# The expert loop of a fused convolution-attention and mixture-of-experts kernel: the small product that moves the second expert's doubled rows, issued in front of the late piece instead of behind it

## The reference

```
x = x + xattn(layernorm(x), k, bias, ctx, ctx, 8)      # long convolution over 512 positions, by head
x = x + moe(layernorm(x))

def moe(x):                                            # T = 512-wide rows
    scores = softmax(xf @ gate_w.T)                    # 64 experts
    topk_w, topk_idx = top_k(scores, 6)
    # each expert gets up to CAP = 128 of the tokens that chose it (gx), in order
    g, u = split(gx @ gate_up_proj)                    # 512 -> 2 * 192
    eo = (silu(g) * u) @ down_proj * buf_w             # 192 -> 512
    routed = zeros.at[buf_tok].add(eo)                 # rows added at their token
    shared = silu(xf @ sg.T) * (xf @ su.T) @ sd.T      # on all tokens, 384 wide
    return routed + shared
```

## Time and profile before

| | |
|---|---|
| time, median of 3 runs | 1144.73 us (1144.46 to 1146.67) |
| the profiled execution, its own time | 1139.92 us |
| its span in the trace | 1137.9 us |
| TensorE products, busy | 1070.9 us, 94% |
| TensorE weight loads, busy | 840.7 us, 74% |
| VectorE, busy | 825.4 us, 73% |
| GpSimd, busy | 744.1 us, 65% |
| ScalarE, busy | 527.3 us, 46% |
| the two products of `c_move` (line 699) | 64 instructions, 390 ns each in the median |
| the late pieces (lines 626 and 640) | 240 and 90 instructions |

### The profile page before, as it was taken

How to read it: one execution, slowest core, us unless ns; L and a number is a source line. 1 busy time by engine, 2 the same in 40 slices (tenths; PEclk the granted TensorE clock), 3 DMA queues, 4 the chain that set the end, 5 groups by cost and what they waited for, 6 DMA issues and landing times.

```text
span 1137.9 us, 17561 instructions
## 1 busy us (share of the span) xinstructions
PE 1070.9 (94%) x5077; PEld 840.7 (74%) x5077; DVE 825.4 (73%) x1414; ACT 527.3 (46%) x951; POOL 744.1 (65%) x436
## 2 busy tenths in 40 slices
PE   3999999999999999999889999999999999999790
PEld 2777777777777778778789998777777776777460
DVE  3799999999999999999589983465555565555360
ACT  4565556556655655564314222444444444444240
POOL 6999999999999999998012333344345435443432
PEclk9999999999999999999999999999999999999895
DMA  6365644554555445552585556899999999999874
GB/s 195 111 175 161 170 129 138 159 164 133 139 161 160 136 140 161 154 147 79 160 238 136 135 140 170 249 291 294 269 301 290 296 281 267 295 276 278 216 177 60
DMA packets 91134, 217.08 MB, mean 191 GB/s; under 512 B 11240, under 2 KB 15656, under 8 KB 90961
## 3 DMA queue, kind: packets, MB, share of 16 engines
q1 hardware_dynamic: 74544, 177.75, 52.7%
q0 software_dynamic: 16544, 38.78, 16.3%
HBM read 164.82 MB, written 52.18 MB: 191 GB/s over the span
## 4 chain that ended last, share of the span: by engine, by line
PE 72%; DMA 15%; issue 4%; POOL 2%; ACT 1%; DVE 1%; POOLq 0%; DVEq 0%; ACTq 0%
PE Y L460 11%; PE Y L462 11%; PE Y L461 11%; PE Y L547 8%; PE Y L667 7%; PE Y L464 5%; DMA out_dram<-pT,idx_i 4%; DMA out_dram<-o,idx_i 4%; DMA out_dram<-w,idx_i 4%; PE DX L483 2%; PE DX L565 2%; PE Y L626 2%; PE OT L565 2%; PE DX L690 2%; PE TA L477 1%
## 5 line engine op out<-in xcount | busy, mean ns | idle before, releaser
L1032 POOL TENSOR_TENSOR ring<-vT,pT 128x1024 f32<-128x1024 f32 x128 | 249.9, 1963 | 11.1 <-ACT vT L783 10.9
L460 PE MATMUL Y<-split,toep 128*128 128x512 f32 x576 | 237.8, 413 | 10.2 <-POOL split L1040 10.2
L1040 POOL TENSOR_TENSOR split<-ring,split 128x1024 fp32r<-128x1024 f32 x96 | 231.7, 2413 | 0.0
L462 PE MATMUL Y<-split,toep 128*128 128x512 f32 x576 | 226.9, 394 | 0.0
L461 PE MATMUL Y<-split,toep 128*128 128x512 f32 x576 | 225.7, 392 | 0.0
L667 PE MATMUL Y<-ring,xT 128*128 128x384 f32 x512 | 190.8, 496 | 0.0
L1207 DVE TENSOR_TENSOR z<-Y,cT 128x1024 f32<-128x1024 f32 x128 | 156.9, 1226 | 26.9 <-PE Y L464 26.1
L1213 DVE TENSOR_REDUCE o<-z 128x128 f32<-128x1152 f32 x128 | 172.2, 1345 | 1.2
L460 PEld LDWEIGHTS Y<-split,toep 128*128 128x128 f32 x576 | 108.8, 189 | 30.6 <-issue 7.9
L789 ACT ACTIVATE split<-ring 128x1024 fp32r<-128x1024 f32 x96 | 100.8, 1050 | 58.8 <-POOL ring L1032 58.8
L462 PEld LDWEIGHTS Y<-split,toep 128*128 128x128 f32 x576 | 108.5, 188 | 24.3
(11 more groups left out here) (163 smaller groups left out, 1878.3 us busy)
## 6 DMA issues: line engine op xcount, KB each, us to landing
ring<-_L_ffn_gate_up_proj_dram SPq DMA_DIRECT2D x64, 768.0 KB
ring<-in_L_ffn_down_proj_dram SPq DMA_DIRECT2D x64, 384.0 KB
gr<-filters SPq DMA_DIRECT2D x32, 512.0 KB, 4.1
stage<-in_x_dram SPq DMA_DIRECT2D x32, 256.0 KB, 5.6
pT<-in_turned_dram SPq DMA_DIRECT2D x32, 256.0 KB, 4.3
cT<-in_turned_dram SPq DMA_DIRECT2D x32, 256.0 KB, 4.2
xr<-in_x_dram SPq DMA_DIRECT2D x32, 256.0 KB, 3.8
xn_rows<-xn SPq DMA_DIRECT2D x32, 256.0 KB, 2.9
```

Of the source, the lines that this page charges most:

```text
L460: pe.matmul(y, high, kv[:, s, 0, a, n], start=(a == 0), stop=False)
L462: last = pe.matmul(y, low, kv[:, s, 0, a, n], start=False, stop=(a == c))
L1032: pool.tensor_tensor(to.rearrange("p (b j i) -> p b j i", i=NH, j=NH), a, d, ALU.mult).then_inc(kvp_ready, 1)
L1040: pool.tensor_tensor(kv[:, s, 1, c, :], kvp[c], kv[:, s, 0, c, :].bitcast(F32), ALU.subtract).then_inc(kv_ready, 1)
```

## The change

In TensorE's `c_iteration`, the call of `c_move` is taken from behind the late piece to in front of it. Nothing else is changed: same instructions, same waits, same buffers, on all engines.

```diff
@@ -711,14 +711,14 @@
                 if e:
                     c_turn_hid(e - 1)
                 c_up(e, 1)
+                if e % 2 and e > 1:
+                    c_move(e // 2 - 1)
                 if part == "gate":
                     late_half(t, 0)
                 if part == "up":
                     late_half(t, 1)
                 if part == "out":
                     late_out(t)
-                if e % 2 and e > 1:
-                    c_move(e // 2 - 1)
                 if e:
                     c_out(e - 1)
                 if turns(e):
```

## The result

Twelve runs of the changed kernel have a median of 1142.27 us (1139.02 to 1146.83), twelve of the kernel before 1142.05 us (1135.85 to 1151.77). The means, 1142.4 and 1142.1 us, are no further apart than the medians, so these runs by themselves show no difference. The comparison of the runs gives a ratio of 1.0059, with a 95% interval of 1.0036 to 1.0083: slower by 0.6%. The ratios compare fast runs only, and a run more than 1.5% above the fastest of its kernel doesn't count as one, so in the second series the 10 longest of the 35 runs of the kernel before are left out and none of the changed one's; over all its runs the medians give 1.0047 and the means 1.0057.

The account below looks back on a forecast made before the run. TensorE's pace, held at times by the add chain, bounds stage C; 21.0 us of waits less 11.0 of gather waits moves TensorE's end 10.0, the last add 3.8; with the chain's 0 to 7.3, +4 us: 1148.7, range 1143.5 to 1153.0.

Parts of the forecast that it names:

- What bounds the kernel: Stage C: TensorE sets the pace, the scatter-add chain holds it at times and ends last.
- The wait: TensorE's move waits for VectorE's low part of the second expert's result: 0.78 us in 27 iterations, 21.0 us.
- The second way of counting: Wait on TensorE from pair periods, 10.71 less 10.08 us: 0.63 us each, 17.0 in all, the low end.
- The rule of the Trainium skill on weight loads pulled ahead of products: TensorE could pull a load ahead of each of 27 waits; the row was against it, so nothing was subtracted.
- The 11.0 us of gather waits go: TensorE's waits for gathered tokens, 9.6 and 1.4 us, vanish because slower TensorE no longer catches up with the add chain.
- +10.0: TensorE's end in stage C moves later by 21.0 - 11.0 = 10.0 us.
- +3.8: By TensorE's path, the last pair's first add goes out at 1127.0 against 1123.18, 3.8 us later.
- The path by the add chain: Scatter-adds from pair 23 on: last pair's first add 0 to 7.3 us late, middle near TensorE's path.
- The sum on the median: The 4 us taken for the profiled execution was put on the median of runs too, giving 1148.7 us.
- rival (2): TensorE's slack hides all waits, result within 0.2%: 0.63 us a wait, end -0.2 us, 1144.5; chance 0.23.
- (1): The add chain ends last, with the 29.07 us and three full pairs: +7.3 us, 1152; chance 0.23.
- (3): Faster: slower TensorE absorbs the add chain's lateness and thinner traffic shortens the chain, 1143.7 or 1141.5 us; chance 0.09.
- (4): The 27 short waits make TensorE's clock fall to 1.2 GHz at times: +10 us or more, 1155; chance 0.03.

Follow-up runs that it names:

- second series: The unedited changed kernel timed again beside the kernel before: 1142.18 against 1136.84 us, ratio 1.0093 (1.0065 to 1.0121).
- profile pair: One profiled execution of each kernel: the changed one took 1139.02 us, 0.9 us less than the one of before.
- second profile of the changed kernel: A further profiled execution of the unedited changed kernel, from its repeat timing: 1147.78 us.
- second half alone: Against the kernel before, the move stands in front of the piece only in iterations 29 to 55 (14 of 27): 1134.81 us, ratio 0.9968.
- first series: The first timing, twelve runs of each kernel: changed 1142.27 us, before 1142.05 us, ratio 1.0059 (1.0036 to 1.0083).
- old order with (3, 6): Kernel before, third group of shared tiles not added in the loop, four tiles added at the end: 1135.79 us, ratio 0.9963.

## Why the prediction was right, and where it was off

- **What bounds the kernel.** Right. TensorE's pace with holds by the add chain is what the runs show: without the adds of nine shared tiles the kernel takes 1122 us, 12.7 less than with them, and its trace has no wait for gathers.
- **The wait, 0.78 us in 27 iterations, 21.0 us.** The mechanism was right in each of the 27, the size a quarter too large: 0.62 and 16.8 us, 0.60 and 16.3 where nothing else holds TensorE. The mis-sized term is the one read from weight loads' starts, without the 0.16 that the work behind gives back. The second way of counting, 0.63 from the period of pairs, stood in the text as the low end and was close. The lesson is to price a wait by the period of the whole loop where both kinds of iteration are in the trace, not by one gap.
- **The rule of the Trainium skill on weight loads pulled ahead of products** ("TensorE: Matmul & The Clock Gate", "Step-by-step: what each phase is for"). The traces after agree with what was taken from the row: the waiting move's loads start at 925.00, 0.12 us behind the low part's end at 924.88. They aren't pulled ahead of the wait.
- **The 11.0 us of gather waits go.** Right in the profile pair; in the second profile of the changed kernel one of 1.9 us is left. TensorE's last move went from 1114.07 to 1119.58, +5.5 where I had +10.0. The smaller wait accounts for 4.2 of the difference. Two more errors nearly cancel: by the distances of its moves the kernel before had lost 12.4 us, not 11.0, and the loop began 1.3 us later in the changed one. The last pair's first add went from 1123.18 to 1122.60, -0.6 where I had +3.8.
- **The path by the add chain.** The term "if the shared tiles' adds behind it take what they took (29.07)" was mis-sized: they took 22.3 us, 7 less, where I had allowed for 6% less. Pair 23's add was at 1032.55 and not 1034.8. These 7 us go far to explain why the chain was not late at the end of that profile. In the second profile it was, by 8.9 us.
- **The sum on the median.** That +4 came near is partly luck. The profiled pair, for which the sum was made, came out at -0.9 us, as rival (2) had it with its 0.63 a wait (TensorE's end +6.0, the end -0.2). The median of the second series came out at +5.3. The step between the two, "I put the same 4 us on it", has no reason in the trace, and no run shows it: how far an execution's waits for the chain hide the change varies from run to run. An error in the wait and one in this step had opposite signs.
- **Rivals.** (1), the chain late by 7 us at the end, didn't come in the first profile (1.1 us) and came in the second (8.9 us), the run of 1147.78 us. (2), all hidden, holds for the profile pair and for the second half alone, and by the medians for the first series, not for the second. (3) was refuted: the fastest run of the changed kernel, 1138.32, is above 61 of the 105 runs of before. (4): the granted clock stayed at 1.00 in the windows from 731 to 1107.

## What to carry to other kernels

A wait that is set in front of covering work costs its length in every round when the path to it starts at the waiting engine itself. If another chain holds that engine now and then, the cost is hidden in part: take the other chain away in an experiment, and the whole price appears (17.3 us here, against 5). Where runs spread by 2%, one profile isn't the mean: two profiles of the same changed kernel have the last adds 1.1 and 8.9 us late. And where they spread unequally, look at what a ratio of selected runs left out.

## What was not expected of the hardware

- Most of the spread comes with the adds of the shared tiles. The kernel before has a standard deviation of 5.0 us with them over 29 runs, and 2.2 without over six; the changed kernel has 2.9 and 1.0, over twelve each. Most scatter-adds that stand in the chain beside weight loads take from 7 to 11 us each (8.91 in the earlier trace rows, 7.02 and 9.37 above), and behind the last loads some 5 (5.08 above). That this difference from run to run is what the time inherits is argued, not shown, as of every kernel but the changed one a single execution was profiled.
- Four accumulating transfers of 256 KB at the end take 14.2 us until the program ends, one takes 7.3, with no other work of an engine beside them.
- Stage C starts at different times in different builds (first move from 730.7 to 737.6 us, the latter in the old order with (3, 6), where nothing ahead of it was changed). That is as much as the differences between kernels here. In that trace part of it arises in stage B: between 570 and 640 us TensorE's products are busy for 64.09 us, where they were for 68.14 before. I did not find why, nor whether it goes with the build or with the run.
